# Scatters, gathers and the last chunk's loads of a decoder layer are issued at other places

## The reference

```python
x = layernorm(x + attn_ref(x))      # conv, minGRU and feed-forward mixer, each behind an rms norm
x = layernorm(x + xattn_ref(x, ctx, ctx))          # 16 heads, causal, softmax over 120 context rows
# the mixture of experts, 16 experts, the best 2 of each token:
router_logits = sigmoid(x @ gate_w + gate_b)
expert_values, expert_indices = top_k(router_logits, k=2)
expert_values = expert_values / sum(expert_values)
all_outputs = einsum(silu(x @ experts_wg) * (x @ experts_wu), experts_wd)
ffn = x + mlp(x, shared_wg, shared_wu, shared_wd) + sum(expert_values * all_outputs[expert_indices])
x = layernorm(x + ffn)
```

## Time and profile before

| | |
|---|---|
| median of 3 runs | 1701.09 us |
| the profiled execution | 1701.68 us, of it span 1699.9 us |
| mean granted TensorE clock | 0.917 |
| busy: PE, PEld | 1362.3 us, 1107.9 us |
| busy: DVE, ACT, POOL | 1107.3 us, 806.5 us, 852.5 us |

### The profile page before, as it was taken

How to read it: one execution, slowest core, us unless ns; L and a number is a source line. 1 busy time by engine, 2 the same in 40 slices (tenths; PEclk the granted TensorE clock), 3 DMA queues, 4 the chain that set the end, 5 groups by cost and what they waited for, 6 DMA issues and landing times.

```text
span 1699.9 us, 34078 instructions
## 1 busy us (share of the span) xinstructions
PE 1362.3 (80%) x11168; PEld 1107.9 (65%) x11168; DVE 1107.3 (65%) x2851; ACT 806.5 (47%) x3111; POOL 852.5 (50%) x1012
## 2 busy tenths in 40 slices
PE   2878787889898887989889888889879888886250
PEld 1667666777677766777667766767667676765240
DVE  3566766676767776677767777677757777665233
ACT  3645454555556454555446454455536454452020
POOL 5343426443555457454755447463665537453535
PEclk9999998999999998999989999999989998997575
DMA  6000000111222211221211202222212212222551
GB/s 197 8 7 8 7 7 22 50 55 57 63 75 60 72 37 57 73 70 54 71 59 58 86 29 75 68 62 68 63 42 83 71 41 71 65 62 81 145 158 52
DMA packets 142895, 105.77 MB, mean 62 GB/s; under 512 B 12352, under 2 KB 137856, under 8 KB 142720
## 3 DMA queue, kind: packets, MB, share of 16 engines
q1 hardware_dynamic: 134528, 86.80, 17.6%
q0 software_dynamic: 8192, 16.79, 3.4%
HBM read 69.99 MB, written 33.55 MB: 61 GB/s over the span
## 4 chain that ended last, share of the span: by engine, by line
PE 36%; DVE 19%; POOL 15%; ACT 15%; issue 11%; SPq 2%; DMA 2%; DVEq 0%; ACTq 0%; POOLq 0%
ACT pr L884 11%; DVE nm L1165 5%; PE sE L532 4%; POOL sorted_x L1566 4%; PE t L391 3%; PE ma L391 3%; DVE pT L1176 3%; POOL pr L1538 2%; POOL gat L1578 2%; POOL rs L1545 2%; PE pvb L573 2%; PE t L395 2%; DVE ys L1336 2%; PE t L396 2%; PE t L397 2%
## 5 line engine op out<-in xcount | busy, mean ns | idle before, releaser
L1538 POOL TENSOR_TENSOR pr<-pr,ri 128x480 f32<-128x480 f32 x256 | 252.3, 994 | 430.2 <-DVE ri L1180 429.1
L884 ACT ACTIVATE pr<-sE,nm 128x120 f32<-128x120 f32 x512 | 178.0, 360 | 405.8 <-DVE nm L1165 405.6
L564 PE MATMUL pvb<-pT,vv 120*64 120x128 f32 x2048 | 146.7, 288 | 69.7 <-DVE pT L1176 68.9
L564 PEld LDWEIGHTS pvb<-pT,vv 120*64 120x64 f32 x2048 | 115.9, 142 | 100.0 <-DVE pT L1176 91.2
L884 ACT ACTIVATE pr<-sO,nm 128x120 f32<-128x120 f32 x512 | 179.4, 383 | 0.0
L532 PEld LDWEIGHTS sE<-kT,qT 64*128 64x128 f32 x1024 | 134.8, 202 | 58.1 <-issue 58.1
L1176 DVE COPY pT<-t 120x512 f32<-120x512 f32 x256 | 165.2, 684 | 5.7 <-PE t L391 4.3
L532 PE MATMUL sE<-kT,qT 64*128 64x120 f32 x1024 | 159.4, 300 | 0.0
L532 PE MATMUL sO<-kT,qT 64*128 64x120 f32 x1024 | 159.4, 300 | 0.0
L1578 POOL DMA_INDIRECT gat<-sorted_y,slot x128 | 135.7, 1060 | 32.6 <-issue 30.1
L1566 POOL DMA_INDIRECT sorted_x<-x,slot x128 | 128.3, 1002 | 47.0 <-issue 35.4
(11 more groups left out here) (326 smaller groups left out, 3479.9 us busy)
## 6 DMA issues: line engine op xcount, KB each, us to landing
wq<-in_w_e SPq DMA_DIRECT2D x232, 128.0 KB, 2.0
sorted_y<-yq SPq DMA_DIRECT2D x64, 256.0 KB
xq<-sorted_x SPq DMA_DIRECT2D x58, 256.0 KB, 2.8
xt<-in_x SPq DMA_DIRECT2D x16, 256.0 KB, 3.0
sorted_x<-yq SPq DMA_DIRECT2D x16, 256.0 KB, 4.1
out_y<-y SPq DMA_DIRECT2D x64, 64.0 KB, 1.6
cT<-in_ctxT SPq DMA_DIRECT2D x16, 240.0 KB, 3.1
sorted_x<-x,slot POOLq DMA_INDIRECT x128
```

Source lines behind the costliest of these rows:

```text
L564: ins = mm(pvb[r * DK:(r + 1) * DK, (k // 2) * T:(k // 2 + 1) * T], vv[:, q, h * DK:(h + 1) * DK], pT[:, 4 * r + k // 2, :], start=True, s ...
L884: ins = f(pr[:, p % RING, r, i, :], score_banks[r][:, i * S:(i + 1) * S], ACT.Exp, bias=nm[:, p % 2, r, i:i + 1], accum_out=rsum[:, p % 2, ...
L1538: GP.tensor_tensor(pr[:, p % RING, r, :, :], pr[:, p % RING, r, :, :], ri[:, p % 2, r, :, :].to_broadcast([P, 4, S]), ALU.mult).then_inc(s ...
```

## The change

What it does, on each engine:

- The pipeline now passes a list of groups for the last stage. Iteration 15 sums groups 10 and 11, one sequence in each slot from 2 on (`sums_in`), and iteration 16 sums none. Before, iteration 16 summed group 11.
- GpSimd issues one scatter in each slot from 2 on in place of two (rows 0 to 7 of the chunk's 16). The other eight stand in the next iteration, between the mixer's residuals and slot 0. The first four gathers of a group stand right behind them; gathers 4, 5 and 6, 7 are in slots 4 and 6. In a slot, the mixer's norm and the attention's norm now stand ahead of the last norm, the gathers and the scatter.
- In iteration 16 GpSimd issues the 16 scatters of the last chunk in one run.
- The last chunk has its own buffers throughout (hf, xt, xz and xm are used as well). SP issues the loads of quads 56 to 59 and all eight x loads, ACT issues the weights of quads 60 to 63, one quad in each even slot of iteration 16, behind `d_tanh`.
- After the loop, gathers, sums and norms go in pairs of sequences: four gathers, then one norm of two sequences (`e_ln2`).

```diff
-        w_last = [wq[0][:], wq[1][:]] + [carve(flat(qT), ...) for i in range(4)] + [carve(flat(kT), ...) for i in range(2)]
+        w_last = [carve(flat(qT), ...) for i in range(4)] + [carve(flat(kT), ...) for i in range(2)] + [carve(flat(hf), ...) for i in range(2)]
+        x_last = [carve(flat(kT), ...) for i in range(3)] + [carve(flat(hT), ...) for i in range(2)] + [xt[:], xz[:], xm[:]]
...
+                if t < G - 1:
+                    body(there(t + 1), there(t), there(t - 1), there(t - 3), [there(t - 5)] if t >= 5 else [])
+                elif t == G - 1:
+                    body(None, t, t - 1, t - 3, [t - 5, t - 4])
+                else:
+                    body(None, None, t - 1, t - 3, [])
+        def sums_in(es, s):
+            if len(es) == 2:
+                return [(es[(s - 2) // SEQ], (s - 2) % SEQ)] if s >= 2 else []
+            return [(es[0], (s - 3) // 2)] if es and s > 1 and s % 2 else []
... SP, iteration 16:
+                if c == G - 1:
+                    for i in range(2):
+                        x_load(QUADS * d + 2 + i)
+                        w_load(QUADS * d + 2 + i)
+                        d_store(QUADS * d + i)
+                    for n in ("scores", "wo", "proj", "attn_sum"):
+                        sp.wait_ge(sem[n], whole(n, G - 1))
+                    sp.wait_ge(sem["a_bank"], whole("a_bank", G - 1))
+                    for i in range(2):
+                        w_load(LAST + i)
+                        d_store(QUADS * d + 2 + i)
+                    for i in range(quads):
+                        x_load(LAST + i)
+                    for i in range(2, 4):
+                        w_load(LAST + i)
+                    return
... ACT:
+            def w_load(n):
+                k = n // quads
+                act.wait_ge(sem["expert"], upto("expert", k))
+                for u in range(QUAD):
+                    e = act.value_load(ei[k % 2][0:1, j:j + 1], min_val=0, max_val=E - 1)
+                    act.dma_start(w_of(n)[:, u, :], src).then_inc(sem[f"wq_last{(n - LAST) // 2}"], 16)
...
+                    if c == G - 1 and s > 1 and s % 2 == 0:
+                        w_load(LAST + 4 + s // 2 - 1)
... GpSimd:
+                if C and c and c % 2 == 0:
+                    for n in range(CHUNK, 2 * CHUNK):
+                        c_scatter(c // 2 - 1, n)
+                if es:
+                    gathers(es, 0, 4)
+                if c == G - 1:
+                    for n in range(2 * CHUNK):
+                        c_scatter(c // 2, n)
+                    return
...
+                    if B and s > LAG and odd:
+                        ln(b, (s - LAG) // 2, 2, mv2[:], ve2[:], rs2[:])
+                    for e, q in sums_in(es, s):
+                        e_ln(e, q)
+                    if len(es) == 1 and s in (4, 6):
+                        gathers(es, s, s + 2)
+                    elif len(es) == 2 and 2 <= s < PAIRS:
+                        gathers(es, 2 * s, 2 * s + 2)
+                    if C and c % 2 and s > 1:
+                        c_scatter(c // 2, s - 2)
... GpSimd, after the loop:
             for e in (G - 4, G - 2):
-                for i in range(2 * SEQ + 1):
-                    for m in range(2):
-                        if i < 2 * SEQ:
-                            e_gather(e + i // SEQ, 2 * (i % SEQ) + m)
-                    if i:
-                        e_ln(e + (i - 1) // SEQ, (i - 1) % SEQ)
+                for j in range(0, 2 * SEQ + 2, 2):
+                    if j < 2 * SEQ:
+                        for n in range(4):
+                            e_gather(e + j // SEQ, 2 * (j % SEQ) + n)
+                    if j:
+                        e_ln2(e + (j - 2) // SEQ, (j - 2) % SEQ)
```

More of the change, by code:

```diff
@@ L191, in layer_kernel @@
         wide = 2 * I + P
[L192 to L195, removed]
+        w_last = [carve(flat(qT), QUAD * wide * i, wide) for i in range(4)] + \
+            [carve(flat(kT), QUAD * wide * i, wide) for i in range(2)] + [carve(flat(hf), QUAD * wide * i, wide) for i in range(2)]
+        x_last = [carve(flat(kT), 2 * QUAD * wide + QUAD * P * i, P) for i in range(3)] + \
+            [carve(flat(hT), QUAD * P * i, P) for i in range(2)] + [xt[:], xz[:], xm[:]]
         hq_last = gin[:, 0:2 * P].rearrange("p (v n) -> p v n", v=2)
@@ L308, in w_load @@
                     sp.wait_ge(sem["expert"], upto("expert", k))
-                if n >= 2 and n < LAST + 2:
+                if n >= 2 and not last(n):
                     sp.wait_ge(sem["d_down"], upto("d_down", 0, n - 2))
@@ L355, in body @@
                         w_load(QUADS * d + i)
-                for i in range(QUADS):
+                if c == G - 1:
[14 more added lines that the diff above has]
+                    return
+                for s in range(2, PAIRS + LAG):
+                    i, odd = (s - 3) // 2, s % 2
                     n = QUADS * d + i if D else 0
-                    if D and (i + 2 < QUADS or d % 2 == 0):
+                    if D and odd and (i + 2 < QUADS or d % 2 == 0):
                         x_load(n + 2)
                         w_load(n + 2)
-                    if D:
+                    if D and odd:
                         d_store(n)
-                    if F_:
-                        e_store(e, i)
+                    for e, q in sums_in(es, s):
+                        e_store(e, q)
             pipeline(body)
[L367 to L372, removed]
             for i in range(quads):
@@ L1411, in body @@
                         d_act(QUADS * d + s // 2 - 1)
[L1412 to L1415, removed]
+                    for e, q in sums_in(es, s - 1):
+                        e_ln3(e, q)
+                    for e, q in sums_in(es, s):
+                        e_sum(e, q)
                     if A:
@@ L1580, in e_gather, with e_ln2, gathers, body @@
                                       ).then_inc(sem[f"gath{q}"], 16)
-            def body(a, b, c, d, e):
-                A, B, C, F_ = a is not None, b is not None, c is not None, e is not None
+            def e_ln2(e, q):
+                pool.wait_ge(sem["ln3_mv"], upto("ln3_mv", e, q + 1))
+                if q:
+                    pool.wait_ge(sem["ln3_out"], upto("ln3_out", e, q - 1))
+                else:
+                    pool.wait_ge(sem["ln3_out"], whole("ln3_out", e - 1))
+                GP.tensor_tensor(ve3[:], mv3[:, :, 1], eps[:, 0:2], ALU.add).then_inc(sem["ln3_eps"], 2)
+                pool.wait_ge(sem["ln3_eps"], upto("ln3_eps", e, q + 1))
+                GP.tensor_tensor(rs3[:], ve3[:], power[:, 0:2], ALU.pow).then_inc(sem["ln3_rstd"], 2)
+            def gathers(es, lo, hi):
+                for j in range(lo, hi):
+                    e_gather(es[j // (2 * SEQ)], j % (2 * SEQ))
+            def body(a, b, c, d, es):
+                A, B, C = a is not None, b is not None, c is not None
                 if B:
```

64 lines of the change are left out of this document (31 added, 33 removed).

## The result

The changed kernel takes 1650.34 us (median of 4 runs, 1645.75 to 1656.81), the kernel before 1700.78 (4 runs, 1700.12 to 1701.42): a ratio of 0.9706, 95% interval 0.9672 to 0.974, or 50 us less. The forecast was 1658, its range 1637 to 1687. The profiled execution is the slowest of the four, 1656.81 us with a span of 1654.5; its own forecast was 1658.3, and its span is 45.4 us shorter than before (1699.9).

What follows compares the result with a forecast made beforehand. The bound was taken as a loop through several engines in written order, POOL owning a seventh. Terms -40 - 3.5 + 19.5 + 4 - 17.7 - 7.3 + 1.6 = -43.4 took 1701.68 to 1658.3; median forecast 1658, range 1637 to 1687.

Steps and rivals of the forecast that it cites:

- Even iterations 6 to 14: Main loop: fewer DMAs in POOL's slots save 8.0 us in each of five iterations, 40 us, bounds 25 to 46.
- Iterations 2 and 4: Early even iterations: fewer scatters in the slots save 3 us and 0.5 us, together 3.5.
- Odd iterations: Run of scatters and gathers ahead of slot 0 delays x and the first scaling: costs 19.5 us, bounds 0 to 50.
- The second item, the late scaling: Odd iterations, slot 0: POOL's scaling comes behind scatters and gathers, making the transposes that need it 3.5 us late.
- Iteration 15: Takes the sums of eight sequences in place of four, with no mixer beside it: costs 4 us, bounds 0 and 14.
- Iteration 16: Last store directly followed by x loads, half the late weights issued by ACT: saves 17.7 us, bounds 10 and 22.
- The quads and groups 12, 13: Tail, first transposes to first gather of group 14: 39.2 us in place of 46.5, saves 7.3, bounds 0 and 15.
- Groups 14, 15: End of the tail: working in pairs of sequences costs 1.6 us, bounds 0 to 4.
- that the loads are bound by the DMA engines: Rival, tail: DMA engines and not issuing limit the loads, only 8 of 23 us saved, 1673 us; chance 8%.
- That the delay in the odd iterations is swallowed: Rival: later slots absorb the delay, costing 0 in place of 19.5 us, 1639 us; chance 12%.
- That the even iterations keep their excess: Rival: excess comes from DVE and queues, so the five save 3 us each, 1683 us; chance 12%.
- The queue that fills up under a run of eight scatters: Rival: GpSimd's software queue fills, x comes late in each odd iteration, kernel slower, 1722 us; chance 5%.

Runs made afterwards that it cites:

- norms_first: The kernel before, with the mixer's and the attention's norms ahead of the DMAs in a slot, DMAs unchanged in number and place: 1663.46 us, ratio 0.9775.
- old_order: The changed kernel with its norms behind the DMAs in a slot, as before: 1655.71 us, ratio 0.9744.
- after_again: The changed kernel itself, unaltered, measured and profiled a second time: 1650.98 us, ratio 0.9713.
- gathers_late: The changed kernel with the first four gathers of an odd iteration behind the first scalings, two and two: 1649.01 us, ratio 0.9698.
- best2: gathers_late with ScalarE's weight loads two and two in each slot, and groups 14 and 15 one sequence at a time: 1641.42 us, ratio 0.9669.
- sp_only: The changed kernel with all 24 late weight loads of the last chunk issued by SyncE, none by ScalarE: 1713.58 us, ratio 1.0065.
- sp_pad: sp_only with 99 needless waits on TensorE ahead of its first matmul: 1658.52 us, ratio 0.9757.

## Why the prediction was right

It was right in sign and size (1658 against 1650), and in most of its terms. Against the profiled execution (which its sum was made for):

- **Even iterations 6 to 14**, forecast -8.0 each, 95.5 us: measured 95.31, -41.7 for the five. But the cause was half told. The step put the saving down to the number of DMAs in a slot and gave the order of the norms no number of its own. norms_first shows -6.1 from the order alone, old_order -7.4 from the number alone. The largest wait that both cut is TensorE's for `xn` (63.6 us in all before, 20 after), which the prediction did not look up.
- **"By itself it can only help"**, said of the order: true of the whole (norms_first, -37 us), but its halves lost 26 to 31 us in the two runs of each, of which the order is shown to be a part only.
- **Iterations 2 and 4**, forecast -3.5: -4.2 and +1.2, -3.0 together (in after_again -4.2 and -0.6).
- **Odd iterations**, forecast 5 x 3.5 + 2.0 = 19.5: iteration 3 +1.7, 5 to 13 together +13.5, in after_again +10.0. The x load came as worked out, 2.26 us behind the last scatter's start in iteration 5, and PE's wait of 2.39 answers to the 2.6. The second item, the late scaling, was over-sized: it should have added 0.9 to make 3.5 and adds 0.42 at TensorE; gathers_late, which removes it, gains 0.5.
- **Iteration 15**, forecast +4: the first transposes for quad 52 come 84.66 us behind the table load, 76.18 before, so +8.5. This is the term that was furthest off. The bounds were 0 and 14, and I took the value next to what the sums cost in iteration 5, though there are twice as many sums and norms here. The new order is not what costs it: with the old one (old_order) the transposes come 87.70 us behind the table load, 3 us later still. What grows between the table load and these transposes is TensorE's wait for `pT`, the transposed probabilities that come from DVE behind POOL's scaling (2.4 us before, 7.5 after), and its busy time for the same matmuls (59.0 to 62.3 us, the granted clock 0.93 before and 0.90 after).
- **Iteration 16**, forecast -17.7: 58.1 us between the first transposes for quad 52 and quad 56 before, 40.0 after, -18.1. First x load 6.8 us ahead of the transposes (forecast 6.46), directly behind the last store.
- **The quads and groups 12, 13**, forecast 39.2: 1619.07 - 1579.98 = 39.1.
- **Groups 14, 15**, forecast 35.5: 1654.5 - 1619.07 = 35.4. Single sequences give back the predicted 1.5 (best2).

Iteration 15 (+4.5 on the forecast) and the odd iterations (-4.3) cancel, which is luck, and the 2 us that remain are those of the even ones. The median lies 6 us below the profiled execution, because executions of this kernel differ by 0.7% (1645.75 to 1656.81) and the profiled one was the slowest, with a granted clock of 0.928 over the span against 0.935 to 0.944 in the others.

Of the rivals: that the loads are bound by the DMA engines, and a second queue gains little, fell. Bytes and buffers being equal, 16 loads moved to ScalarE are worth 6.0 us (204.70 to 198.72), and between the first transposes for quads 52 and 56 the DMA share rose from 0.50 (142 GB/s) to 0.71 (209), so the DMA engines had room before. The Trainium skill's rule that issuing from several engines only saves sequencer time (DMA: Bandwidth & Descriptors, section Issuing engines are not separate DMA queues) names the mechanism rightly; "usually small" does not hold here, where one issue takes about 0.9 us (four in 3.64) and 16 stand in a row. That the delay in the odd iterations is swallowed is partly true: 15.1 of the 19.5 stayed, 11.4 in after_again. That the even iterations keep their excess, or that the odd ones lose 8.3 us, is answered by the windows (95.31 and 93.84). The queue that fills up under a run of eight scatters did not show: 2.25 to 2.48 us from the last scatter's start to the x load in iterations 3, 5, 7, 9 and 13, and 4.04 in 11 (2.58 in after_again).

## What to carry to other kernels

On an engine that both computes for others and issues DMAs, put the computations that someone waits for ahead of the issues of its slot, and all of them: here both together gained 37 us, while with only one kind moved the wait came back at the kind left behind, and both kernels were slower (for reasons that are not all known). Before pricing a slot by its number of DMAs, read who waits for the engine's results and for how long: two edits that remove the same wait do not add up. When one engine issues a long row of loads, look at what stands behind them in its queue: here it was the stores, and the buffers that they free. Where an engine takes over DMA issues in a chain, spread them over its idle times two and two rather than four in a row (here 1.05 us a quad).

## What was not expected of the hardware

- Stalls of 2 to 12 us that no instruction in the trace explains, seen in the four kernels that ran together on one chip and in none of the others. In sp_only TensorE went on with one instruction per 0.7 to 2.1 us while VectorE stood still for 6.79 us and GpSimd's DMA instructions kept their 1.27 us. In sp_only they came back at the same place of each odd iteration from 5 to 13, and the kernel took 55 us more than sp_pad, its twin without them; in the other three they lie mainly in the even iterations. Chip or program is open. A kernel that suddenly costs 3% more in code that was not touched should be run again elsewhere before it is explained.
- A long wait can have an aftermath: behind the stall in slot 0 of sp_only, TensorE's granted clock stood at 0.50 from 915 to 920 us, after 1.00 until 913, so that the work behind it ran at 1.2 in place of 2.4 GHz:

```profile
907.00:909.00 2.00, 1.31 (x9) 0.71 (x6) 0.00 (x0) 1.14 (x2) 1.56 (x2) 1.00 0.19 61
...
913.00:915.00 2.00, 0.73 (x2) 0.21 (x2) 1.17 (x3) 0.00 (x0) 0.86 (x1) 0.56 0.01 4
915.00:920.00 5.00, 3.60 (x16) 3.20 (x16) 3.66 (x8) 3.82 (x18) 1.93 (x2) 0.50 0.58 161
```
